# Context and first weights loaded by both queues, each for 64 of the 128 partitions

## What is computed

```python
Q = (img_embed @ Wq).reshape(B, -1, H, D).transpose(0, 2, 1, 3)
K = (sent_embed @ Wk).reshape(B, -1, H, D).transpose(0, 2, 1, 3)
V = (sent_embed @ Wv).reshape(B, -1, H, D).transpose(0, 2, 1, 3)
score = jnp.einsum('bhqd,bhkd->bhqk', Q, K) / math.sqrt(D)
mask = (atten_mask != 0)[:, None, None, :]
score = jnp.where(mask, score, -jnp.inf)
attn = jax.nn.softmax(score, axis=-1)
ctx = jnp.einsum('bhqk,bhkd->bqhd', attn, V).reshape(B, -1, H * D)
out = ctx @ Wo + img_embed
...
return (out - mu) * jax.lax.rsqrt(var + EPS) * gamma + beta
```

## Time and profile before

| what | value |
|---|---|
| time, median of 3 runs | 355.78 us (355.52 to 356.03) |
| the profiled execution's own time | 354.91 us |
| its span, first to last instruction | 353.1 us |
| mean granted TensorE clock | 0.999 of full |
| TensorE busy | 347.5 us, 98% of the span |
| VectorE, ScalarE, GpSimd busy | 265.1, 228.6, 193.0 us |
| DMA, whole span | 55.80 MB, mean 158 GB/s |

### The profile page before, as it was taken

One profiled execution on the slowest core, in us unless ns is written; L12 is line 12 of the kernel. 1 busy time (PEld: TensorE's weight loads), 2 busy tenths in 40 slices (PEclk: granted clock), 3 DMA queues, 4 the chain that ended last, 5 costly groups with the idle time before them and its releaser, 6 DMA issues. The chain is left out here.

```text
span 353.1 us, 6783 instructions
## 1 busy us (share of the span) xinstructions
PE 347.5 (98%) x2272; PEld 323.9 (92%) x2272; DVE 265.1 (75%) x495; ACT 228.6 (65%) x778; POOL 193.0 (55%) x208
## 2 busy tenths in 40 slices
PE   9999999999999999999999999999999999999994
PEld 6999999999999999998899899988988998899884
DVE  2159998673921277898798988987988989879896
ACT  3267764244333569887876976878768769778560
POOL 0045640000003857679679688687696796885243
PEclk9999999999999999999999999999999999999999
DMA  8999779775735070052242341541522413403003
GB/s 236 425 420 337 255 240 338 274 250 211 228 137 202 0 278 22 3 179 97 84 151 70 137 152 38 172 137 43 180 90 91 149 65 144 148 32 120 32 35 114
DMA packets 19682, 55.80 MB, mean 158 GB/s; under 512 B 1728, under 2 KB 3264, under 8 KB 17728
## 3 DMA queue, kind: packets, MB, share of 16 engines
q1 hardware_dynamic: 18784, 54.38, 42.8%
q10 hardware_dynamic: 864, 1.00, 1.1%
HBM read 46.98 MB, written 8.39 MB: 157 GB/s over the span
## 5 line engine op out<-in xcount | busy, mean ns | idle before, releaser
L646 PE MATMUL pair<-vw_hi,pt_hi 128*128 128x512 f32 x155 | 62.2, 402 | 0.0
L646 PE MATMUL pair<-vw_hi,pt_lo 128*128 128x512 f32 x155 | 60.9, 393 | 0.0
L646 PE MATMUL pair<-vw_lo,pt_hi 128*128 128x512 f32 x155 | 60.5, 391 | 0.0
L1250 POOL TENSOR_TENSOR out_sb<-centred,beta_sb 128x512 f32<-128x512 f32 x30 | 38.8, 1294 | 28.9 <-ACT centred L840 28.8
L1270 POOL TENSOR_TENSOR x_sum<-xt_in 128x256 f32<-128x256 f32 x16 | 11.9, 745 | 62.2 <-DMA xt_in<-x_tiles 62.1
L795 ACT ACTIVATE prob<-c,neg_max 128x77 f32<-128x77 f32 x128 | 44.0, 346 | 0.0
L1295 POOL TENSOR_TENSOR xo_lo<-x_sum,xo_hi 128x512 fp32r<-128x512 f32 x32 | 41.6, 1304 | 0.5 <-ACT xo_hi L819 0.5
L571 PE MATMUL pair<-a_hi,xo_hi 128*128 128x308 f32 x128 | 40.4, 316 | 0.0
L571 PE MATMUL pair<-a_hi,xo_lo 128*128 128x308 f32 x128 | 38.9, 304 | 0.0
L571 PE MATMUL pair<-a_lo,xo_hi 128*128 128x308 f32 x128 | 38.9, 304 | 0.0
L833 ACT ACTIVATE pt_hi<-pair 128x640 fp32r<-128x640 f32 x32 | 22.5, 703 | 23.5 <-PE pair L633 23.5
(11 more groups left out here) (119 smaller groups left out, 945.0 us busy)
## 6 DMA issues: line engine op xcount, KB each, us to landing
w_out<-wo SPq DMA_DIRECT2D x8, 1024.0 KB, 4.8
xt_in<-x_tiles SPq DMA_DIRECT2D x16, 512.0 KB, 3.8
x_in<-x_rows SPq DMA_DIRECT2D x16, 512.0 KB, 4.8
out<-out_sb SPq DMA_DIRECT2D x31, 256.0 KB, 2.2
w_out<-wq_t SPq DMA_DIRECT2D x7, 1024.0 KB, 7.8
w_proj<-wv SPq DMA_DIRECT2D x8, 768.0 KB, 4.7
w_proj<-wk SPq DMA_DIRECT2D x6, 768.0 KB, 9.6
w_out<-wq_t SPq DMA_DIRECT2D x2, 512.0 KB, 7.9
```

Of the source, the lines that this page charges most:

```text
L646: mm = pe.matmul(ps_out[:, i % 2, 0:s.model], ps[:, j, :], v[:, b, j, :], start=(j == 0 and n == 0), stop=(j == s.key_t - 1 and n == len(p ...
L1250: pool.tensor_tensor(out_sb[i % OUT_RING][:, :], centred[i % 2][:, :], beta_sb[:, :], ALU.add)\
```

## The change

Context and the four tiles of use 0 are each loaded by two DMAs, partitions 0 to 63 (`UPPER`) from SP and 64 to 127 (`LOWER`) from ACT, so that both queues carry context, tile 0, tile 1, tile 2, tile 3 in this order. Two DMAs now add to one semaphore, and what waits for the context or for a tile of use 0 waits for 32 in place of 16. The tiles of use 1 stay whole and divided between the queues as before. The mask goes from the end of ACT's issues to SP, behind the tiles of use 1 and ahead of use 0's `w_out`. Of the eight idle products one has 256 columns in place of 512.

```diff
-    WARM_UP = 8
+    WARM_UP = 7
+    UPPER, LOWER = slice(0, P // 2), slice(P // 2, P)
...
                 if u == 0:
-                    for m in range(1, s.dim_t, 2):
-                        sp.dma_start(tile_cols(w_proj_sb[0], m), tile_cols(src, m)).then_inc(ld_first[m], DMA_INC)
+                    for m in range(s.dim_t):
+                        sp.dma_start(tile_cols(w_proj_sb[0], m)[UPPER], tile_cols(src, m)[UPPER])\
+                          .then_inc(ld_first[m], DMA_INC)
...
-            sp.dma_start(ctx_sb[:, :, :], ctx_t).then_inc(ld_ctx, DMA_INC)
+            sp.dma_start(ctx_sb[UPPER, :, :], ctx_t[UPPER]).then_inc(ld_ctx, DMA_INC)
             load_w_proj(0)
             for u in range(USES):
                 if u + 1 < USES:
                     load_w_proj(u + 1)
+                if u == 0:
+                    sp.dma_start(mask_sb[:, :], mask.rearrange("b k -> (b k)").partition_broadcast(P))\
+                      .then_inc(ld_mask, DMA_INC)
...
-                        pe.wait_ge((ld_first, ld_second)[u][m], DMA_INC)
+                        pe.wait_ge((ld_first, ld_second)[u][m], (2, 1)[u] * DMA_INC)
...
-
-            pe.wait_ge(ld_ctx, DMA_INC)
+            pe.matmul(pairs[3][:, 0, 0:COLS], ones[:, 0:P], ones[:, 0:COLS], start=True, stop=True)
+
+            pe.wait_ge(ld_ctx, 2 * DMA_INC)
...
-            for w, ld, to in ((wk[0], ld_first, w_proj_sb[0]), (wk[1], ld_second, w_proj_sb[1])):
-                for m in range(0, s.dim_t, 2):
-                    act.dma_start(tile_cols(to, m), tile_cols(w, m)).then_inc(ld[m], DMA_INC)
-            act.dma_start(mask_sb[:, :], mask.rearrange("b k -> (b k)").partition_broadcast(P)).then_inc(ld_mask, DMA_INC)
+            act.dma_start(ctx_sb[LOWER, :, :], ctx_t[LOWER]).then_inc(ld_ctx, DMA_INC)
+            for m in range(s.dim_t):
+                act.dma_start(tile_cols(w_proj_sb[0], m)[LOWER], tile_cols(wk[0], m)[LOWER])\
+                   .then_inc(ld_first[m], DMA_INC)
+            for m in range(0, s.dim_t, 2):
+                act.dma_start(tile_cols(w_proj_sb[1], m), tile_cols(wk[1], m)).then_inc(ld_second[m], DMA_INC)
...
-                act.wait_ge(ld_ctx, DMA_INC)
+                act.wait_ge(ld_ctx, 2 * DMA_INC)
```

## The result

The changed kernel takes **358.02 us** (median of six executions, 357.29 to 358.20); the kernel before, beside it on the same chip, 355.57 (355.31 to 356.03). The ratio is 1.0065, 95% interval 1.0055 to 1.0076: 2.45 us slower. The forecast was 356.1, and its range ended at 357.3.

The account below looks back on a forecast made before the run. TensorE, 98% busy, was taken as bound at 23.8 us by use 3's weights landing. Profiled 354.91 + 0.35 (mask) = 355.26, plus 0.87 to the median, gave 356.1 us; 8-in-10 range 355.4 to 357.3.

Parts of the forecast that it names:

- More DMAs: Context and use 0, 10 DMAs instead of 5: extra issues on ACT and SP covered by waits and backlog, cost 0.
- I take the lead as reached: At the first product: tile 0 lands early enough for TensorE to begin at 4.04 instead of 4.25 us.
- First loads in order of need: Context and tile 0: both queues carry tile 0 before tile 1, landing it up to 0.2 us sooner, nearer 3.93.
- The idle products: At TensorE's start: half an idle product less lets it begin 0.21 us earlier, worth -0.1 us (0 to -0.2).
- The mask's new place: Mask on SP's queue: everything behind it lands +0.35 us later, the middle between 0 and 0.75.
- The sum's carrier: At 23.8 us: use 3's weights land 0.35 us later, delaying ACT, POOL and TensorE equally, kept to the end.
- the sum's 0.87 us: Whole kernel: the profiled execution lies 0.87 us under the median 355.78, taken as the same for both kernels.
- Rival 2: Early loads: half the partitions, half the rate; everything behind context and use 0 lands 2.7 us later, 358.5 us; 16%.
- its sign to watch for: DMA rate from 2.5 to 6.5 us: near 375 GB/s, or near 190 if half the partitions halve the rate.
- The port rule: DMAs to SBUF: partitions 0 to 63 reach only 8 of 16 ports; cited for the half-rate case, held at 16%.
- Rival 3: TensorE's start: late data and a stand-still delay the higher clock level, costing 1.65 us less 0.1 slack, 357.3 us; 6%.

Follow-up runs that it names:

- the first loads alone: Kernel before, mask's load at use 6, seven and a half idle products, only context and tile 0 halved between queues: by rows 356.20 us, by 64 partitions 358.05 us.
- seven and a half idle products: Kernel before with seven and a half idle products in place of eight, all loads and queues as before: 355.55 us.
- mask late: Kernel before with the mask's load put off to use 6, issued by SP: 355.50 us.
- large whole tiles: Kernel before with use 0's two `w_out` DMAs made four of one whole 128-partition tile each, same queue: 355.71 us.
- large even and odd halves: Kernel before with use 0's two `w_out` DMAs made four, for even or odd partitions, same queue: 355.74 us.
- the large loads: Kernel before with use 0's two `w_out` DMAs made four: lower and upper 64 partitions 357.42 us, even and odd 355.74, whole tiles 355.71.
- filling the pause alone: The change with eleven and a half idle products in place of seven and a half, keeping TensorE busy until tile 0 lands: 357.54 us.
- the first loads by rows: Kernel before, mask's load at use 6, seven and a half idle products, only context and tile 0 cut into halves of rows: 356.20 us.

## Why the prediction was wrong

**The step that failed** is "More DMAs", where it says "Cost 0. If half a DMA issues faster, it is 0 too", and with it "I take the lead as reached" under the loads in order of need. Ten halves of 64 partitions are not free: they took the early stream from 375 to 213 GB/s and tile 0 from 4.11 to 5.52, and the kernel lost 2.45 us. The same ten DMAs cut by rows lost 0.6.

Half a DMA does not issue faster but slower: 0.57 us against 0.38 for the context. So ACT's table load came at 5.31 where the prediction had 4.0, and use 2's weights were issued at 6.66 instead of 5.4. One tile each 0.46 us on two queues offered 2 x 197 KB / 0.46 us = 855 GB/s, far above the 375 that the engines took; halves of 98 KB at 0.62 and 0.70 us (2.49 and 2.80 for four) offer 98 / 0.62 + 98 / 0.70 = 298 (KB of 1000 bytes). With these issue times "Cost 0" could not hold.

But slow issues are not the whole of it. The 213 measured lie a good deal under the 298, and the DMA engines stood partly idle while more than 1 MB was issued and not moved. The ten DMAs by rows, four in 1.84 us on SP and in 1.91 on ACT, offer 98 / 0.46 + 98 / 0.48 = 417, and moved 267. Of the 1.5 us by which tile 0 lands later by partitions than by rows in the first loads alone, 0.6 go with the issue. The share accounts for 0.74 / 1.05 = 0.70 of the rate, and a longer time for each byte for the rest, 0.80 (213 / 375 = 0.57 = 0.70 x 0.80). That longer time is not one of every packet: the median packet of 1536 bytes takes 65 ns in both traces, but from 2.5 to 6.5 us 29 of 447 in the change took over twice as long, up to 0.93 us, and 13 of 875 before, up to 0.46 us.

**First loads in order of need.** The context came earlier (3.6), tile 0 not: 5.5, where the prediction had it between 3.93 and 4.14. The same DMAs by rows land it at 3.87, so the order itself does what the prediction said, and the cut by partitions undoes it.

**The idle products.** The term of -0.1 us is 0: alone, they change nothing (ratio 1.0000).

**The mask's new place.** Predicted +0.35 for what stands behind it, measured +0.37 at use 3's weights, when moved alone. The near match is not shown to be more than luck, since the same weights land at 19.46 with the mask left in its place and seven and a half idle products. In the changed kernel the term is not on the path: TensorE is later there than those weights.

**The sum's carrier.** "It is the landing of use 3's weights that sets TensorE's time" held for the profiled execution of before; with the mask late these weights came 1.8 us earlier and the time did not move. ACT began to round them at 19.16 all the same, behind work of 18.84 that had waited for TensorE. In that run the same 48 passes, without a pause ahead of them, take 7.22 us instead of 6.65, with 11 of them from 4.2 to 6.2 us where before had 15: the higher level came later. Then TensorE is behind the weights by itself. The profiled execution of before was one with an early level. Five profiled executions of kernels that can't be told apart in time show what that is worth: the products with `w_out` start at 10.74 us (before), 11.02 (large whole tiles), 11.29 (mask late), 11.49 (large even and odd halves) and 11.61 (seven and a half idle products), and these executions took 354.91, 355.36, 355.58, 355.71 and 355.84 us. What TensorE has lost by then, by a later level or a later start, stays to the end. So the sum's 0.87 us for a profiled execution under the median, "the same for both kernels", was no constant either: the changed kernel's lay 0.13 above its median.

**Rival 2** named half the partitions, a lower rate, and 358.5. Size and sign fit (358.02), and so do the late landings; its sign to watch for, the rate from 2.5 to 6.5 us, showed it. What it says first, that such a DMA may not fill the engines, is the share of 0.74. The port rule that it cites is not the reason here: with even and odd partitions, for which the large loads showed no loss, the change is as slow. What that rule describes exists, for two halves that follow one another on one queue. The Trainium skill (DMA: Bandwidth & Descriptors, Rules for kernel authors) advises one transfer for 128 partitions because two halves share the same 16 engines. The advice holds here, though the engines were partly idle.

**Rival 3**, the clock: it happened, TensorE at the lower level until 9.7 us, but filling the pause alone gave back 0.36 us, with overlapping intervals.

What stays open is why small DMAs of 64 partitions take longer to issue and to land, and what holds the rate at 213 to 236 GB/s, below what their issues offer. The shape of a DMA alone does not set its issue time: in the change the first whole tile behind the halves on SP's queue still took 0.59 us to issue, and the next one 0.43. That halves of rows also lose 0.6 us behind an early tile 0, and the first loads by rows 0.7 with four halves and no early mask, says that cutting small DMAs has a price of its own; it was not taken apart further.

## What to carry to other kernels

Share an early load between two queues by whole tiles, not by partitions. Halves of rows bring one tile sooner, but here the next tile came later and the kernel lost 0.6 to 0.7 us. Before costing more and smaller DMAs at nothing, compare what the issues offer (bytes by issue time, over the queues) with the rate that the engines take; it is an upper bound, and the rate here fell below it. And a load that binds in one profiled execution may not bind in the median: the same kernel with that load taken away shows it.

## What had not been expected

- A DMA for 64 partitions takes longer to issue than one for 128: 0.57 us against 0.38 for the context, 0.62 against 0.46 for a tile, and the same for even and odd partitions.
- 64 neighbouring partitions cost 71 us of engine time for each MB where 128 partitions, or 64 even ones, cost 39, when one half follows the other on one queue. With both halves under way at once full engines moved 358 GB/s.
- With eight idle products and no pause, the level of TensorE's clock still rises at different times from execution to execution: 48 passes took 6.65 us in one and 7.22 in another, and the time of the kernel followed.
- The longer time for each byte in the change comes from single packets of up to 0.93 us; the median packet of 1536 bytes takes 65 ns as before.
